# The softmax row sums of a long cross attention: who adds the tiles of the first seven heads

## The reference

```
q = (x @ Wq)  k = (context @ Wk)  v = (context @ Wv)      # per head: q 1024x64, k and v 6404x64
attn = softmax(q @ k.T * 64 ** -0.5, axis=-1)             # 1024 x 6404 per head
out = (attn @ v) joined over heads @ Wo + bo
```

## Time and profile before

| | |
|---|---|
| median of 3 runs | 1381.0 us (1378.33 to 1384.72) |
| the profiled execution | 1381.02 us |
| its span | 1379.2 us |
| span less PE's busy time | 28.2 us |
| POOL busy | 965.3 us (70%) |
| DVE busy | 983.3 us (71%) |
| ACT busy | 826.8 us (60%) |

### The profile page before, as it was taken

One profiled execution on the slowest core, in us unless ns is written; L12 is line 12 of the kernel. 1 busy time (PEld: TensorE's weight loads), 2 busy tenths in 40 slices (PEclk: granted clock), 3 DMA queues, 4 the chain that ended last, 5 costly groups with the idle time before them and its releaser, 6 DMA issues.

```text
span 1379.2 us, 19972 instructions
## 1 busy us (share of the span) xinstructions
PE 1351.0 (98%) x6335; PEld 782.9 (57%) x6335; DVE 983.3 (71%) x1413; ACT 826.8 (60%) x1631; POOL 965.3 (70%) x556
## 2 busy tenths in 40 slices
PE   9999998799999999999999999999999999999998
PEld 7777776534545555554554555554555555555864
DVE  8966566578887667676767777677767666776765
ACT  5468886465565656656665655656665655555731
POOL 5201112413899999999999999899999999998210
PEclk9999999979999999999999999999999999999999
DMA  7630000400000200200020020002002000001100
GB/s 211 209 108 17 17 18 8 94 5 2 1 1 0 60 0 1 52 9 1 1 59 1 0 52 8 1 1 59 2 1 49 9 1 0 9 0 56 57 0 16
DMA packets 77884, 41.40 MB, mean 30 GB/s; under 512 B 63822, under 2 KB 69599, under 8 KB 77511
## 3 DMA queue, kind: packets, MB, share of 16 engines
q1 hardware_dynamic: 77798, 40.28, 11.5%
HBM read 26.53 MB, written 13.74 MB: 29 GB/s over the span
## 4 chain that ended last, share of the span: by engine, by line
PE 94%; DVE 4%; ACT 1%; issue 1%; DMA 1%; DVEq 0%; ACTq 0%; SPq 0%
PE ps L1626 26%; PE ps L1613 15%; PE ps L1614 14%; PE ps L1573 9%; PE ps L1560 3%; PE ps L1848 2%; PE ps L1397 2%; PE ps L1433 2%; PE ps L1434 2%; PE ps L1435 2%; PE ps L1424 2%; PE ps L1423 2%; PE ps L1422 2%; DVE probs L1146 1%; PE ps L1829 1%; PE ps L1830 1%
## 5 line engine op out<-in xcount | busy, mean ns | idle before, releaser
L639 POOL TENSOR_TENSOR psums<-psums,probs 126x1024 f32<-126x1024 f32 (+1 forms) x392 | 821.4, 2096 | 66.5 <-ACT probs L852 11.2
L852 ACT ACTIVATE probs<-ps 126x512 f32<-126x512 f32 (+1 forms) x816 | 412.7, 625 | 256.3 <-PE ps L1614 242.4
L1086 DVE TENSOR_REDUCE chunk_max<-ps 128x2 f32<-128x1008 f32 (+1 forms) x364 | 415.5, 1183 | 153.3 <-PE ps L1573 153.0
L1626 PE MATMUL ps<-probs,v_mem 126*64 126x512 f32 (+1 forms) x1632 | 389.8, 598 | 0.0
L1613 PE MATMUL ps<-q_heads,ring 128*126 128x512 f32 (+1 forms) x816 | 334.2, 410 | 0.5
L1614 PE MATMUL ps<-q_low,ring 128*126 128x512 f32 (+1 forms) x816 | 321.3, 394 | 0.0
L1626 PEld LDWEIGHTS ps<-probs,v_mem 126*64 126x64 f32 (+1 forms) x1632 | 111.6, 136 | 173.4 <-issue 124.0
L789 ACT CAST ring<-ps 64x252 fp32r<-64x252 f32 (+1 forms) x356 | 128.1, 360 | 117.7 <-PE ps L1560 114.6
L1613 PEld LDWEIGHTS ps<-q_heads,ring 128*126 128x126 f32 (+1 forms) x816 | 151.2, 185 | 80.6 <-issue 44.1
L1180 DVE TENSOR_TENSOR xn<-xn,probs 126x512 f32<-126x512 f32 x126 | 176.9, 1404 | 24.1 <-ACT probs L852 18.9
L1614 PEld LDWEIGHTS ps<-q_low,ring 128*126 128x126 f32 (+1 forms) x816 | 152.0, 186 | 31.7
(11 more groups left out here) (242 smaller groups left out, 1517.4 us busy)
## 6 DMA issues: line engine op xcount, KB each, us to landing
v_scratch<-v_stage SPq DMA_DIRECT2D x51, 252.0 KB
v_mem<-v_scratch SPq DMA_DIRECT2D x8, 1606.5 KB
ctx_mem<-in_ctx_t SPq DMA_DIRECT2D x3, 803.2 KB, 9.0
vslot<-in_ctx_rows SPq DMA_DIRECT2D x51, 47.2 KB
xn<-rden_scratch SPq DMA_DIRECT2D x14, 128.0 KB
pair_w<-in_f_pairs SPq DMA_DIRECT2D x1, 1351.0 KB, 11.7
pair_w<-in_f_pairs SPq DMA_DIRECT2D x1, 965.0 KB, 8.7
pair_w<-in_f_pairs SPq DMA_DIRECT2D x1, 579.0 KB, 6.5
```

What stands on the lines that cost most here:

```text
L639: pool.tensor_tensor(sums[0:r, 0:width], sums[0:r, 0:width], probs[0:r, n % PROBS, 0:width], ALU.add).then_inc(c_sum, 1)
L852: act.activation(probs[0:r, n % PROBS, cols(half)], ps[0:r, score_bank(t, half), :], ACT.Exp, scale=float(HD) ** -0.5).then_inc(c_exped, 1)
L1086: dve.tensor_reduce(chunk_max[:, h % 2, i:i + 2, c], ps[:, banks[0]:banks[1] + 1, 0:group_tiles(c) * KT], AX, ALU.max).then_inc(c_reduced, 1)
L1626: ins = pe.matmul(ps[half * HD:(half + 1) * HD, B_ACC, :], v_tiles[0:r, h % 2, t, :], probs[0:r, n % PROBS, cols(half)], start=(t == 0), s ...
```

## The change

In heads 0 to 6, GpSimd adds all 1,024 columns of every tile; VectorE adds nothing there, and the add that joined both parts is gone. Head 7 is as before. The waits on VectorE's adds in these heads go too, and the semaphore values are counted anew.

```diff
 def adds_to(h, t):
-    return TILES * h + max(t, 1)
+    return (TILES - 1) * h + max(t, 1)

 def by_vector(h, t):
-    return h == HEADS - 1 or t % GT == GT - 1
+    return h == HEADS - 1

 def vector_done(h, t):
-    before = h * (TILES // GT)
-    return before + (max(t, 1) if h == HEADS - 1 else (t + 1) // GT)
+    return max(t, 1) if h == HEADS - 1 else 0

 def vector_adds(h, t):
-    before = h * (TILES // GT)
-    return before + (max(t, 1) if h == HEADS - 1 else t // GT + 1)
+    return vector_done(h, t)
...
                         pool.tensor_tensor(sums[0:r, 0:width], sums[0:r, 0:width], probs[0:r, n % PROBS, 0:width],
                                            ALU.add).then_inc(c_sum, 1)
-                if h < HEADS - 1:
-                    pool.wait_ge(c_sum, adds_to(h, TILES - 1))
-                    pool.wait_ge(c_sumd, vector_done(h, TILES - 1))
-                    pool.tensor_tensor(sums[:, HALF:TOK], sums[:, HALF:TOK], psums_v[:, h % 2, :], ALU.add).then_inc(c_sum, 1)
...
             def add_rows(h, t):
-                first = 1 if h == HEADS - 1 else GT - 1
+                first = 1
...
-                    if h < HEADS - 1 and b:
-                        add_rows(h, b * GT - 1)
...
             def sum_rows(h):
-                pe.wait_ge(c_sum, adds_to(h, TILES - 1 if h == HEADS - 1 else TILES))
-                pe.wait_ge(c_sumd, vector_done(h, TILES - 1))
+                pe.wait_ge(c_sum, adds_to(h, TILES - 1))
+                if h == HEADS - 1:
+                    pe.wait_ge(c_sumd, vector_done(h, TILES - 1))
```

## The result

The changed kernel takes 1431.07 us (median of 4 runs, 1429.55 to 1432.44), the kernel before 1382.72 us in the same comparison. The ratio is 1.0371 with a 95% interval of 1.035 to 1.0392: slower. The forecast was 1434. The profiled execution took 1432.09 us with a span of 1430.2 us.

A forecast was written before the change was run, and what follows sets the result against it. GpSimd's adds, level with TensorE before, were to bound heads 0 to 6: 329.0 + 880.3 + 8.2 + 17 + 1.4 = 1235.9 us. With 53 us passed on, 1381 + 53 = 1434 us; range 1422 to 1450 us.

The forecast's parts named there:

- rival C: Heads 0 to 6: TensorE's long blocks and GpSimd's surplus don't overlap, both bounds in series; 1444 us, chance 4%.
- Step 1: Heads 0 to 6: 350 GpSimd adds at 2.372 + 0.143 us, 880.3 us; upper bound the present mean, 2.42 us.
- Step 2: GpSimd's other work in heads 0 to 6: six `normalize` 8.2 us, twelve `queries_lo` 17 us; joining add gone.
- Step 3: GpSimd's start in head 0: 1.4 us of waiting at tile 4, from 337.9 us on always work.
- The ring: `probs` buffer of two blocks: ScalarE may run one to two blocks ahead; used up within head 0 or 1.
- Step 4: End of head 6's last add: 1235.9 us against 1182.03 before, GpSimd 53.9 us later.
- Step 5: Head 7, bound by TensorE: block 1's exponentials wait for head 6's last add, +53.5 us less 0.5: +53 us.
- Step 6: VectorE loses 78 adds and 7 copies, 115.9 us busy; gain at most 4.8 us, under GpSimd's bound nothing.
- A: Heads 0 to 6: `probs` buffers and TensorE's heavier blocks hide the longer adds; 1376 to 1383 us, chance 3%.
- E: Cheaper GpSimd adds, 2.32 us each; 1416 us, chance 3%.
- D: TensorE's clock falls as it stops shortly: one block in twenty at 1.2 GHz, 34 us; 1468 us, chance 3%.
- the prediction's last sign of being wrong: The prediction is wrong if TensorE's clock falls; it was to stay at 1.00 throughout.

The follow-up runs named there:

- experiment 3: TensorE multiplies only 256 of each 512 tokens with the values (tiles 1 to 49): 1426.64 us from the changed kernel, 1369.55 us from the kernel before.
- experiment 4: From the kernel before, GpSimd adds whole tiles and VectorE keeps its adds too, not joined in heads 0 to 6: 1458.64 us, ratio 1.0581.
- narrowed changed kernel: The changed kernel, but TensorE multiplies only 256 of each 512 tokens with the values for tiles 1 to 49: 1426.64 us.
- kernel that makes one of two adds: From the kernel with two tiles per block to VectorE (1481.08 us), VectorE makes only one of the two adds: 1377.39 us, ratio 0.9977.

## Why the prediction was right, step by step

- *What bounds (GpSimd level with TensorE).* Right, shown by experiment 3: with TensorE 13 us a head lighter the kernel before kept its 121 us in heads 1, 2, 3, 5 and 6. But two readings on the way, and a product, were wrong. The six waits of ScalarE that the view puts down to GpSimd were not for it. One of them:

```profile
356.94 3.19 ACT L852 ACTIVATE probs<-ps 126x512 f32<-126x512 f32 x6 [2.49 <-POOL psums L639]
```

  This is block 3 of head 0. The add that it needs, that of tile 7, ended at 337.90 + 8.82 = 346.72 us, 10.2 us earlier. So the second reading, "nearly always behind with its adds and catches up just in time" does not fit: GpSimd had no free time, but what ScalarE needed of it was always ready, and the argument of rival C from these waits had no ground. And 55 x 0.13 is 7.2 us, not 7.4; the gap is 0.135 us.
- *Step 1, 2.372 us an add.* Measured 2.376 (x336), without VectorE's adds beside them. The rejected price of 2.42 belongs to a mix with VectorE's adds; experiment 4 brings it back (2.446).
- *Step 2.* `queries_lo` fell to 1.27 us as assumed (1.452 and 1.327 before).
- *Step 3.* One wait of 1.54 us, 1.4 expected. The ring is used up by the start of head 1, as written. But the exponentials do not start with GpSimd "every time": in heads 1 to 6 they do in 8 to 10 of the 13 blocks, and in blocks 2 to 4 of each head TensorE is the later one. GpSimd has work in these too, so the sum does not feel it.
- *Step 4.* End of head 6's adds 1235.1 us, 1235.9 expected; 0.3 us of the difference is an earlier start (328.71 against 328.98).
- *Step 5.* ScalarE starts block 1 of head 7 at 1235.11 us, straight after that add: 52.6 us later than before (53.5 expected). The 0.5 us that I subtracted did not come: block 1 takes 1243.62 - 1235.11 = 8.51 us, as long as before. And from there to the end the span is 1.6 us shorter than before (186.6 against 188.2 us), where the prediction allowed 1 us. It lies behind the attention and not in the change: to the last add of head 7 both take 81.2 us. The clock accounts for it. The stretches from that add to the end, first before (with four us of it), then after; the granted clock is the last figure but two:

```profile
1272.20:1379.20 107.00, 102.36 (x442) 71.43 (x438) 68.30 (x177) 44.45 (x79) 13.92 (x20) 0.98 0.10 34
1277.00:1281.00 4.00, 4.00 (x14) 3.26 (x13) 3.83 (x22) 1.28 (x2) 1.10 (x2) 0.57 0.95 343
```

```profile
1324.80:1430.20 105.40, 100.75 (x442) 70.32 (x438) 68.31 (x177) 44.45 (x79) 13.92 (x19) 1.00 0.10 35
```

  A mean of 0.57 over 4 us is 1.7 us of full clock lost, by my estimate, and TensorE is busy 1.6 us longer with the same 442 instructions.
- *Step 6.* TensorE's wait for VectorE fell from 4.8 to 0.8 us and bought nothing.
- *Sum.* The span grew by 51.0 us, 53 expected. In the medians the growth is 48.4 us, because the median of before lies 1.7 us above its profiled run and that of the changed kernel 1.0 us below its own.
- *The lock.* Where I weighed the exclusive lock against the 0.26 us, I read the row wrongly; the last section shows it. The sum did not rest on it.
- *Rivals.* A needed an add of 2.17 us; none came. C fell with experiment 3. E needed 2.32 us. D: the granted clock was 1.00 from 329 to 1220 us with TensorE 95% busy, and fell once, at the end of head 6, after TensorE had idled 2.7 of the 3 us from 1222 on:

```profile
1225.00:1229.00 4.00, 4.00 (x10) 1.93 (x12) 2.50 (x2) 3.32 (x7) 3.86 (x2) 0.57 0.01 4
```

  By the letter that is the prediction's last sign of being wrong; it cost nothing, since GpSimd still held the stage until 1235 us. In the narrowed changed kernel, with TensorE 85% busy, the clock did go up and down, 1.00 in most stretches of 10 us and 0.83 and 0.84 in those from 630 and 670 us, 0.97 in the mean. The section "A second HAM failure mode: psum-queue depth-cycling" of the Trainium skill ("TensorE: Matmul & The Clock Gate") describes such a clock for a kernel whose TensorE idles shortly and often; the narrowed kernel agrees, the changed one at its load does not.

## What to carry to other kernels

An engine whose instructions wait for each other has no free time well below 100% busy: add the gap between two of its instructions (0.14 us here) to each before calling the rest free. Price an operation from rows without the neighbour that the change removes, not from the mean of all. Don't take the view's releaser for the one that held an instruction before its own time has been looked up. And work handed between GpSimd and VectorE has no fixed price: the same 512-column add took VectorE 0.67 to 2.9 us, in the mean 1.41 in one kernel and 2.35 in another, by how much of GpSimd's add beside it was still to come. So a split that is balanced by busy time can tip over when either list shifts.

## What the runs showed of the hardware that was not expected

- The contention is a lock, and its price is set by when the two adds start. In the kernel with two tiles per block on VectorE, GpSimd's and VectorE's timelines (start, us):

```profile
645.85 2.41 POOL L639 TENSOR_TENSOR psums<-psums,probs 126x1024 f32<-126x1024 f32 x1 [2.20 <-ACT probs L852]
...
648.40 2.61 POOL L639 TENSOR_TENSOR psums<-psums,probs 126x1024 f32<-126x1024 f32 x1
```

```profile
646.61 4.95 DVE L1180 TENSOR_TENSOR xn<-xn,probs 126x512 f32<-126x512 f32 x2
```

  and in the kernel before, around the add of the earlier trace rows, which starts at 601.92:

```profile
600.49 1.29 POOL L639 TENSOR_TENSOR psums<-psums,probs 126x512 f32<-126x512 f32 x1
```

```profile
600.82 1.51 DVE L1180 TENSOR_TENSOR xn<-xn,probs 126x512 f32<-126x512 f32 x1
```

  VectorE's pair ends at 651.56, 0.55 us after GpSimd's second add (651.01); the single one ends at 602.33, 0.55 us after GpSimd's half add (601.78). So an add of VectorE gets through only when the GpSimd add beside it ends, and the next GpSimd add, which has started 0.14 us after that end, takes 0.26 us longer. Counted over heads 0 to 6, VectorE's add ends within 0.02 us of 0.55 us after the GpSimd add beside which it started in 71 of 78 cases before, 59 of 79 in experiment 4 and 155 of 162 with two tiles per block. So it takes 0.55 us plus what is left of GpSimd's add when it starts. Whether that one is whole or half is not what counts: before, 45 of the 78 started beside a whole add, and in experiment 4 nearly all did; with two tiles per block the median add started with 2.1 us of GpSimd's still to come. The others start in the last 0.15 us of a GpSimd add, or they came first, before GpSimd's add or up to 0.8 us after its start. Then VectorE's add takes 0.67 to 0.69 us, and where it came first GpSimd's is up to 1.3 us longer. VectorE's and GpSimd's in the kernel that makes one of two adds:

```profile
552.57 0.69 DVE L1179 TENSOR_TENSOR xn<-xn,probs 126x512 f32<-126x512 f32 x1
```

```profile
552.79 2.73 POOL L638 TENSOR_TENSOR psums<-psums,probs 126x1024 f32<-126x1024 f32 x1 [0.92 <-ACT probs L851]
```

  The Trainium skill, "SBUF — State Buffer", section "Who interferes with whom", states just that exclusive lock; these rows agree, but for the cases in which VectorE got in first though GpSimd's add, by the profile's rough starts, already ran. The prediction took the 0.26 us as a sign against it. It is no sign, since most of VectorE's add falls into the gap and the start of the next.
- VectorE's reductions did not slow GpSimd, as the same section says: in the changed kernel the 27 full adds of 126 partitions with no VectorE instruction beside them took 2.378 us in the mean, the 185 with nothing but reductions beside them 2.379 us.
- Two float32 products whose outputs lie in different 64 partitions run side by side: 16 instructions and 8 both took 3.58 us.
